# Attention heads of the first and second pass in pairs on two halves of the TensorE array, with one mask product for each bank

## What is computed

```python
H = 16; D = C // H                       # 16 heads of 8 numbers
q, k = apply_rope(q, cos, sin), apply_rope(k, cos, sin)
att = jnp.einsum('bhtd,bhsd->bhts', q, k) * scale
att = jnp.where(causal, att, -inf)
att = jax.nn.softmax(att, axis=-1)
y = jnp.einsum('bhts,bhsd->bhtd', att, v)
```

## Time and profile before

| what | value |
|---|---|
| time, median of 3 runs | 2073.77 us (2073.59 to 2076.99) |
| the profiled execution | 2074.39 us, span 2072.6 us |
| TensorE busy | 1816.3 us (88%), 11328 matmul records |
| TensorE weight loads busy | 881.0 us (43%) |
| VectorE busy | 1580.1 us (76%) |
| ScalarE busy | 1273.3 us (61%) |
| GpSimd busy | 1047.0 us (51%) |
| mean granted TensorE clock | 0.967 of 2.4 GHz |
| chain that ended last | PE 64%, DVE 13%, ACT 10%, POOL 6%, DMA 3% |

### The profile page before, as it was taken

How to read it: one execution, slowest core, us unless ns; L and a number is a source line. 1 busy time by engine, 2 the same in 40 slices (tenths; PEclk the granted TensorE clock), 3 DMA queues, 4 the chain that set the end, 5 groups by cost and what they waited for, 6 DMA issues and landing times.

```text
span 2072.6 us, 32651 instructions
## 1 busy us (share of the span) xinstructions
PE 1816.3 (88%) x11328; PEld 881.0 (43%) x11328; DVE 1580.1 (76%) x2934; ACT 1273.3 (61%) x2803; POOL 1047.0 (51%) x1124
## 2 busy tenths in 40 slices
PE   1658999989999898989999998999999899998775
PEld 0223443535444353535444453544435354443332
DVE  4538787888878788788888888887878888787461
ACT  0335757576675757566675756667575766758461
POOL 1223556363645646374655636465563636455433
PEclk8879999999999999999999999999999999999986
DMA  3231203112121302113120211213021121200000
GB/s 97 48 36 32 37 29 43 35 26 30 37 37 42 36 30 33 23 37 36 42 37 30 40 33 27 33 39 37 29 44 35 26 29 37 36 17 14 11 1 6
DMA packets 87617, 68.71 MB, mean 33 GB/s; under 512 B 10720, under 2 KB 83104, under 8 KB 87328
## 3 DMA queue, kind: packets, MB, share of 16 engines
q1 hardware_dynamic: 87456, 66.62, 17.5%
HBM read 32.51 MB, written 10.49 MB: 21 GB/s over the span
## 4 chain that ended last, share of the span: by engine, by line
PE 64%; DVE 13%; ACT 10%; POOL 6%; DMA 3%; issue 3%; SPq 0%; POOLq 0%; DVEq 0%; ACTq 0%; PEldq 0%
PE Y L463 11%; PE M L556 5%; POOL Z L1069 5%; PE S2a L428 5%; ACT Pq L683 5%; PE S1c L404 5%; PE S2b L428 4%; DVE nmaxF L848 4%; PE M L593 3%; PE S1b L404 3%; PE M L514 3%; PE M L489 3%; DMA Ks<-parts 3%; DVE ztmp L930 3%; PE Y L454 2%
## 5 line engine op out<-in xcount | busy, mean ns | idle before, releaser
L1069 POOL TENSOR_TENSOR Z<-Z,ztmp 128x1280 f32<-128x1280 f32 x112 | 324.5, 2897 | 327.9 <-DVE ztmp L958 326.8
L1036 POOL TENSOR_SCALAR_AFFINE_SELECT PT<-PT 128x256 f32<-128x256 f32 (+1 forms) x640 | 254.5, 409 | 386.6 <-ACT PT L668 383.5
L1060 POOL TENSOR_TENSOR Vf<-Vf,ztmp 128x512 f32<-128x512 f32 x256 | 349.0, 1363 | 102.2 <-DVE ztmp L930 93.6
L668 ACT ACTIVATE PT<-S2a 128x512 f32<-128x512 f32 x320 | 191.6, 599 | 170.6 <-PE S2a L422 166.2
L463 PE MATMUL Y<-PT,Vf 128*64 128x512 f32 x1024 | 274.8, 617 | 0.0
L672 ACT ACTIVATE PT<-S2a 128x512 f32<-128x512 f32 x256 | 153.6, 600 | 158.5 <-PE S2a L428 155.7
L930 DVE TENSOR_TENSOR ztmp<-xv,wv_s 128x512 f32<-128x512 f32 x256 | 238.0, 930 | 2.8 <-POOL Z L1069 2.8
L404 PE MATMUL S1c<-Kf,Qf 64*128 64x512 f32 x352 | 203.6, 659 | 36.2 <-ACT Pq L683 32.2
L404 PE MATMUL S1a<-Kf,Qf 64*128 64x512 f32 x352 | 204.5, 662 | 20.6 <-ACT Pq L683 20.6
L668 ACT ACTIVATE PT<-S2b 128x512 f32<-128x512 f32 x320 | 191.5, 598 | 26.3 <-PE S2b L422 26.0
L404 PE MATMUL S1b<-Kf,Qf 64*128 64x512 f32 x320 | 182.8, 652 | 9.5 <-ACT Pq L683 9.5
(11 more groups left out here) (108 smaller groups left out, 3760.7 us busy)
## 6 DMA issues: line engine op xcount, KB each, us to landing
Qs<-parts SPq DMA_DIRECT2D x96, 128.0 KB
Ks<-parts SPq DMA_DIRECT2D x96, 128.0 KB
tab_s<-in_tab SPq DMA_DIRECT2D x16, 512.0 KB, 4.5
...
```

The lines of the kernel that those rows point to most:

```text
L668: nc.scalar.activation(PT[:, slot % 2, b, :], t[:, :], ACT.Exp, scale=SCALE_A).then_inc(exps_done.sem, 1)
L1036: last = nc.gpsimd.affine_select(out=v, in_=v, compare_op=ALU.is_ge, fill=0.0, base=0, pattern=pattern, channel_multiplier=-1)
L1060: nc.gpsimd.tensor_tensor(Vf[:, i, :, :], Vf[:, i, :, :], vtmp[:, n % VBUF, :, :], ALU.add).then_inc(v_acc.sem, 1)
L1069: nc.gpsimd.tensor_tensor(Z[:, :, :, :], Z[:, :, :, :], ztmp[:, hh % 2, :, :, :], ALU.add).then_inc(z_acc.sem, 1)
```

## The change

In `Qs` and `Ks` even heads now stand at partitions 0 to 49 and odd heads at 64 to 113 (48 rows of parts, two of maxima or ones), eight heads deep instead of sixteen. The host orders the columns of the weights and tables so that the parts of even heads come out on partitions 0 to 63. A matmul of either pass has 48 or 50 rows, on the array's rows 0 to 63 or 64 to 127. `pass1` and `pass2` of the attention do two banks at an even step and nothing at the odd one. The banks are in pairs whose first bank has an even head and whose second an odd head; the banks of 256 + 256 columns are the last two of a group. In pass 1 one mask product covers both diagonal blocks of a bank. Both banks must be free first, so the waits are for one bank later than before. Each scatter DMA is cut in two, one for even and one for odd heads.

```diff
-    for pair in range(GA // 2):
-        h0, h1 = 2 * pair, 2 * pair + 1
-        for h in (h0, h1):
-            BANKS_A1 += [[(h, 3, 0)], [(h, 2, 0), (h, 0, 384)]]
-            BANKS_A2 += [[(h, 0, 0)], [(h, 1, 0), (h, 3, 384)]]
-        BANKS_A1.append([(h0, 1, 0), (h1, 1, 256)])
-        BANKS_A2.append([(h0, 2, 0), (h1, 2, 256)])
+    for h0 in range(0, GA, 2):
+        BANKS_A1 += [[(h, 3, 0)] for h in (h0, h0 + 1)] + [[(h, 2, 0), (h, 0, 384)] for h in (h0, h0 + 1)]
+        BANKS_A2 += [[(h, 0, 0)] for h in (h0, h0 + 1)] + [[(h, 1, 0), (h, 3, 384)] for h in (h0, h0 + 1)]
+    BANKS_A1 += [[(h, 1, 0), (h + 2, 1, 256)] for h in (0, 1)]
+    BANKS_A2 += [[(h, 2, 0), (h + 2, 2, 256)] for h in (0, 1)]
...
                         for r in range(NSP):
-                            sp.dma_start(dst[DA * r:DA * r + DA, :, :],
-                                         parts[:, qk, order[r], :]).then_inc(scattered.sem, 16)
+                            for lo in (0, HALF):
+                                sp.dma_start(dst[lo + DA * r:lo + DA * r + DA, :, :],
+                                             parts[lo:lo + HALF, qk, order[r], :]).then_inc(scattered.sem, 16)
...
-                    if group >= SA and b % GF:
+                    if b % 2:
                         return
...
-                    pe.wait_ge(*s1_free(j, (n if group < SA else n + 1) - len(S1)))
+                    pe.wait_ge(*s1_free(j, n + 1 - len(S1)))
                     if group < SA:
-                        for h, qt, col in BANKS_A1[b]:
-                            hh, keys = GA * group + h, (qt + 1) * P
-                            nc.tensor.matmul(t[:, col:col + keys], Qs[0:ROWS_P1, hh, qt * P:keys],
-                                             Ks[0:ROWS_P1, hh, 0:keys], start=True, stop=False)
-                            last = nc.tensor.matmul(t[:, col + qt * P:col + keys], identb[:, :], maskb[:, :],
-                                                    start=False, stop=True)
-                        last.then_inc(s1_filled.sem, 1)
+                        for i in range(2):
+                            for first, (h, qt, col) in enumerate(BANKS_A1[b + i]):
+                                hh, keys, r = GA * group + h, (qt + 1) * P, HALF * (h % 2)
+                                nc.tensor.matmul(S1[(n - 1 + i) % len(S1)][:, col:col + keys],
+                                                 Qs[r:r + ROWS_P1, hh // 2, qt * P:keys],
+                                                 Ks[r:r + ROWS_P1, hh // 2, 0:keys], start=first == 0, stop=False)
+
+                        for i in range(2):
+                            t, segs = S1[(n - 1 + i) % len(S1)], BANKS_A1[b + i]
+                            blocks = t[:, :].rearrange("p (k c) -> p k c", c=P)
+                            blocks = (blocks[:, 3:4, :] if len(segs) == 1 else blocks[:, 1::2, :]
+                                      if segs[0][1] == segs[1][1] else blocks[:, 2:4, :])
+                            nc.tensor.matmul(blocks, identb[:, :], maskb2[:, 0:len(segs), :],
+                                             start=False, stop=True).then_inc(s1_filled.sem, 1)
...
-                    pe.wait_ge(exps_done.sem, exps_done.at(j, n - len(S2)))
+                    pe.wait_ge(exps_done.sem, exps_done.at(j, (n + 1 if slot < SA else n) - len(S2)))
                     if slot < SA:
-                        for h, kt, col in BANKS_A2[b]:
-                            hh = GA * slot + h
-                            last = nc.tensor.matmul(t[:, col:col + T - kt * P], Ks[0:ROWS_P2, hh, kt * P:kt * P + P],
-                                                    Qs[0:ROWS_P2, hh, kt * P:T], start=True, stop=True)
+
+                        for i in range(2):
+                            for h, kt, col in BANKS_A2[b + i]:
+                                hh, r = GA * slot + h, HALF * (h % 2)
+                                last = nc.tensor.matmul(S2[(n - 1 + i) % len(S2)][:, col:col + T - kt * P],
+                                                        Ks[r:r + ROWS_P2, hh // 2, kt * P:kt * P + P],
+                                                        Qs[r:r + ROWS_P2, hh // 2, kt * P:T], start=True, stop=True)
+                            last.then_inc(s2_filled.sem, 1)
```

More of the change, by code:

```diff
@@ L38, in attention_and_mixture @@
     NSP = len(SPLITS_Q)
-    ROWS_P1 = 96
+    ROWS_P1 = NSP * DA
     ROWS_P2 = ROWS_P1 + 2
+    HALF = 64
     HF, DF, E = 8, 64, wo.shape[0] // 64
@@ L305, in rows @@
                     sp.wait_ge(*drained(j, f"rows{group}"))
-                    for i in range(2):
-                        sp.dma_start(Qs[ROWS_P1 + i:ROWS_P1 + i + 1, GA * group:GA * group + GA, :],
-                                     mrowA[i * GA * NT:(i + 1) * GA * NT, :]).then_inc(rowsA_in.sem, 16)
+                    for odd in range(2):
+                        r = HALF * odd + ROWS_P1
+                        sp.dma_start(Qs[r:r + 2, GA // 2 * group:GA // 2 * (group + 1), :],
+                                     mrowA[odd * GA * NT:(odd + 1) * GA * NT, :]).then_inc(rowsA_in.sem, 16)
                 if f_end:
@@ L409, in pass2 @@
                     t = S2[(n - 1) % len(S2)]
+                    if slot < SA and b % 2:
+                        return
                     if not (a if slot < SA else f):
@@ L429, in pass2 @@
                                                        ident[:, :])
-                    last.then_inc(s2_filled.sem, 1)
+                        last.then_inc(s2_filled.sem, 1)
                 def has_values(slot):
@@ L653, in _ @@
             nc.scalar.activation(identb[:, :], ident[:, :], ACT.Copy).then_inc(consts_cast.sem, 1)
-            nc.scalar.activation(maskb[:, :], maskf, ACT.Copy).then_inc(consts_cast.sem, 1)
+            for i in range(2):
+                nc.scalar.activation(maskb2[:, i, :], maskf, ACT.Copy).then_inc(consts_cast.sem, 1)
             def iteration(j, a, f, f_end, a_prep, f_prep):
@@ L837, in maxima @@
                         if len(segs) == 2 and segs[1][1] == qt0:
-                            last = nc.vector.tensor_reduce(nmaxA[:, GA * group + h0:GA * group + h0 + 2, qt0],
+                            last = nc.vector.tensor_reduce(nmaxA[:, h0 % 2, GA // 2 * group:GA // 2 * (group + 1), qt0],
                                                            t[:, :].rearrange("p (h k) -> p h k", h=2), AX.X, ALU.max,
@@ L842, in maxima @@
                             for h, qt, col in segs:
-                                last = nc.vector.tensor_reduce(nmaxA[:, GA * group + h, qt:qt + 1],
+                                last = nc.vector.tensor_reduce(nmaxA[:, h % 2, GA // 2 * group + h // 2, qt:qt + 1],
                                                                t[:, col:col + (qt + 1) * P], AX.X, ALU.max, negate=True)
@@ L1132 @@
         cos, sin = np.cos(ang), np.sin(ang)
-        tabs.append(np.stack([np.repeat(np.concatenate([cos, cos]), H, 0), np.repeat(np.concatenate([-sin, sin]), H, 0)], 1))
+        rows = [np.tile(np.repeat(np.concatenate(t), H // 2, 0), (2, 1)) for t in ((cos, cos), (-sin, sin))]
+        tabs.append(np.stack(rows, 1))
     Wv, Wo = np.asarray(L0_ffn_Wv), np.asarray(L0_ffn_Wo)
```

33 lines of the change are left out of this document (17 added, 16 removed).

## The result

The changed kernel takes 2088.8 us (median of 7 runs, 2079.6 to 2090.5); the kernel before took 2075.3 us in the runs beside it. The ratio is 1.006, with a 95% interval from 1.0043 to 1.0077: slower by 0.6%. The forecast was 2087 us.

The account below looks back on a forecast made before the run. Bound taken: TensorE in slots 6, 7, 0, POOL's Z chain in slot 1, the mixture's maximum-exponential-fill loop in slots 2 to 5. Profiled 2074.4 + 2 (iterations) + 6 (clock) + 5 (start, end) = 2087.4, forecast 2087 us; range 2060 to 2119.

Parts of the forecast that it names:

- Switch 0.09: Each change of TensorE between whole and divided array, as between scores and masks, costs 0.09 us (bounds 0 and 0.10).
- A pair of split banks gains nearly nothing, by its order: Scores of two banks of 384 + 128 columns: three successive steps and two weight loads, 0.41 us where 0.45 stood.
- Slots 6, 7 and 0, -0.4: Up to slot 0's last pair: savings on half-array scores less added switches, together -0.4 us an iteration.
- The new wait, +1.15: Slot 0 to 1: pass 2 waits for bank 9's exponential, so POOL's Z chain and slot 1's end come 1.15 us later.
- Slots 2 and 3, -0.6: Mixture slots: fewer switches and bank b+1 filled ahead of the projections; together -0.6 us an iteration.
- The clock, +6: Behind the wait for Z: low clock in four more iterations, 1.6 us each, +6 us in all (bounds 0 to 22).
- Start and end, +5: First iterations and the end: 2 us lost on banks DVE must read, 3 us where ACT paces pass 2.
- the scatter, 0: 24 DMAs instead of 12, same bytes, hidden in steady state; at the start taken as 0 us, bounds -6 and +8.
- Cheap switches: Rival: switches between two bf16 forms need not drain the array; 2069 us at half price, 2051 at none; chance 0.20.
- Loads like f32: Rival: 0.07 us more for some 30 weight loads in slots 6, 7, 0 and slot 1's stretch; 2119 us; chance 0.12.
- halves one after the other: Rival: the array's two halves do not run side by side in bf16; +47, 2134 us; chance 0.06.
- No net effect: Rival: switches cost 0.09, but the clock falls no more often and the start costs less; 2074 to 2079 us; chance 0.20.

Follow-up runs that it names:

- e4: The changed kernel with each mask product made as two 64-row products on its bank's own half of the array; 2091.7 us, ratio 1.0064.
- e1: The changed kernel with the matmuls of two banks of two segments issued head by head in both passes; 2085.3 us, ratio 1.0038.
- e2: The kernel before with only the pairing, bank order and one mask product per bank, scores still on the whole array; 2114.3 us, ratio 1.0174.
- e3: The changed kernel with DVE's second product for Z after the maximum of bank 4, not 3, in slots 0, 1, 6, 7; 2109.1 us, ratio 1.0150.
- e6: e5 with DVE's second product for Z behind the maximum of bank 4 instead of 3 in slot 7 alone; 2066.6 us, ratio 0.9947.
- e5: The changed kernel with POOL's two additions into Z in slot 1 behind its masks of banks 1 and 2, not 2 and 4; 2082.4 us, ratio 1.0016.
- e9: e6 with pass 2 of slots 2 and 3 bank by bank again, in pairs only in slots 0 and 1; 2078.2 us, ratio 1.0001.
- e10: e9 with ACT's copy of Y behind the exponential of bank 9 instead of bank 8 in slots 0 and 1; 2080.1 us, ratio 1.0015.
- e12: e6 with ACT's copy of Y behind the exponential of bank 9 in slots 0 and 1; 2051.7 us, ratio 0.9867.

## Why the prediction was right where it was

The sum holds because two errors of opposite sign in one of its steps nearly cancel, and the shape of the cost there was not foreseen. By its own steps:

- *Prices.* Switch 0.09: 0.10 measured, and e4, which has neither the switch nor the 0.10 at these places, shows that it is the switch. Loads of bf16 weights on one half 0.02: nothing that shows. Halves side by side: yes. "A pair of split banks gains nearly nothing, by its order" was wrong: 0.23 us instead of 0.41, since the halves do not wait for each other in the program's order (e1), and 0.23 instead of 0.37 for the pair of 256-column banks. With eight split pairs and two others up to bank 8's scores that is 8 x 0.18 + 2 x 0.14 = 1.7 us an iteration that the sum lacked; 23 switches at 0.10 take 0.2 of it back. By these prices 1.7 us would come off the work, and 1.4 do.
- *Slots 6, 7 and 0, -0.4.* Measured +0.42, the step that failed. The work fell by 1.4 us (forecast 0.17) and the cover of the wait for ySB is right (0.50 instead of 0.73 us), but 2.0 us of waits for S1's banks stood against it. The text counted such a wait only at the start and, with 0.7 us, in slot 1; that TensorE must find two of three banks free in slots 7 and 0 too, behind DVE's products, it did not price. e2, e3 and e6 show it. Two errors of opposite sign, 1.2 us of work and 2.0 us of waits, thus left the sum near; that is luck, not foresight.
- *The new wait, +1.15.* Measured +1.03: 5.34 us where 5.46 were worked out. The pair waits 0.79 us for bank 9's exponential behind ACT's copy, after 0.35 for S1, 1.14 together where about 1.1 was forecast. From pass 2 of bank 2 to Z it is 7.89, as forecast by POOL's chain, and e5 shows that the chain ends the slot. TensorE's idle time at Z was put at 2 us: 1.57, since 1.10 were spent at S1 before.
- *Slots 2 and 3, -0.6.* -1.04. e2 gives 0.3 to the pairing and 0.7 to the halves; by e9 the pairing in pass 2 is worth 1.3 once the halves are there.
- *The clock, +6.* +7.2: behind Z in four more iterations, as forecast, and at the end of slot 3 in two instead of one. The other runs show how loosely this count hangs on the change, so that its agreement may be chance.
- *Start and end, +5; the scatter, 0.* +3.0 together, 2.7 less at the start and 5.7 more at the end. The data of the scatter are waited for 28.6 us instead of 42.5, and what that and the shorter clearing brought (8.6 us at the first scores) went into 9 us more up to the first transposes, mostly at the lower clock. In slots 4 and 5 it is hidden, 29.11 us as before.
- *Rivals.* Cheap switches: no, 0.10. Loads like f32, halves one after the other: no. No net effect: no, the interval of the ratio lies above 1.

What stays open is when the clock falls. It followed idle time behind Z and at the end of slot 3, more often where two waits lay close (e3), but e10, with less idle time ahead, lost to it what it had won, and e4 and e12 did not; e2 with somewhat shorter waits and more work has it once. None of the runs changed the idle time by itself.
